# Gathering table rows by index without a bound on the indices

## The reference

```
h = feats * rsqrt(deg_out)[:, None]
m = segment_sum(h[src], dst, num_segments=n) * rsqrt(deg_in)[:, None]
x = (m @ W_gc + b_gc) + (feats @ W_res + b_res)
core = top-2 mixture of 64 experts, 256 -> 512 -> 256, over x
y = x + core
out = layernorm(feats + batchnorm(y) * gamma + beta)
```

## Time and profile before

| | |
|---|---|
| Median of 3 runs | 3077.5 us (3076.79 to 3083.35) |
| The profiled execution: its time | 3077.82 us |
| Its span, first to last instruction | 3076.0 us |
| Mean granted clock of TensorE | 0.826 of full speed |
| First and last start of a gather at L465 | 217.4 and 2259.5 us |
| First and last start of a gather at L490 | 2298.2 and 2863.2 us |

### The profile page before, as it was taken

How to read it: one execution, slowest core, us unless ns; L and a number is a source line. 1 busy time by engine, 2 the same in 40 slices (tenths; PEclk the granted TensorE clock), 3 DMA queues, 4 the chain that set the end, 5 groups by cost and what they waited for, 6 DMA issues and landing times.

```text
span 3076.0 us, 44225 instructions
## 1 busy us (share of the span) xinstructions
PE 2073.9 (67%) x10214; PEld 1715.2 (56%) x10263; DVE 1252.8 (41%) x3095; ACT 396.0 (13%) x1350; POOL 2030.9 (66%) x1989
## 2 busy tenths in 40 slices
PE   7955555565666666666667667677758898989370
PEld 7944344454444444555555555555647787989350
DVE  9971112122222333444444445555551222222467
ACT  1010000000000000000101111111112222322013
POOL 2017777777777777777777777777744677777603
PEclk6557877778788888888888899998988999999785
DMA  8033333333333333333333333333323465666332
GB/s 285 0 99 102 102 101 101 102 103 103 103 104 103 105 103 105 105 105 105 106 105 105 107 107 107 107 107 107 108 78 121 154 194 179 200 184 192 111 118 83
DMA packets 205321, 362.69 MB, mean 118 GB/s; under 512 B 43336, under 2 KB 126070, under 8 KB 205054
## 3 DMA queue, kind: packets, MB, share of 16 engines
q0 software_dynamic: 93888, 230.63, 26.0%
q1 hardware_dynamic: 104058, 123.31, 12.7%
q10 hardware_dynamic: 7108, 6.43, 0.6%
HBM read 328.57 MB, written 57.52 MB: 126 GB/s over the span
## 4 chain that ended last, share of the span: by engine, by line
POOL 45%; PE 21%; issue 19%; DVE 6%; DMA 4%; DVEq 2%; POOLq 1%; ACT 1%; PEld 1%; ACTq 0%; SPq 0%; PEldq 0%
POOL ring L465 22%; POOL stage L465 22%; PE bank L1270 7%; PE bank L1264 6%; PE bank L1135 3%; PE bank L1155 3%; DMA ring<-nodes,slots 2%; DVE acc L1048 1%; PE bank L1257 1%; DMA stage<-y 1%; PE bank L1195 1%; DVE stage L757 1%; PEld bank L1342 1%; PE bank L1174 0%; DVE srcT L1087 0%
## 5 line engine op out<-in xcount | busy, mean ns | idle before, releaser
L465 POOL DMA_INDIRECT ring<-table,ring_idx x792 | 790.8, 999 | 242.1 <-issue 240.9
L465 POOL DMA_INDIRECT stage<-table,ring_idx x776 | 774.5, 998 | 236.4 <-issue 235.2
L1155 PE MATMUL bank<-ring,hot 128*128 128x257 f32 x1056 | 310.4, 458 | 181.7 <-DMA ring<-table,ring_idx 166.1
L1155 PE MATMUL bank<-stage 128*128 128x257 f32 x1040 | 307.4, 460 | 166.3 <-DMA stage<-table,ring_idx 155.8
L1155 PEld LDWEIGHTS bank<-ring,hot 128*128 128x128 f32 x1056 | 241.2, 234 | 244.9 <-issue 158.2
L1155 PEld LDWEIGHTS bank<-stage 128*128 128x128 f32 x1040 | 238.8, 235 | 229.8 <-issue 155.1
L953 DVE TENSOR_TENSOR acc<-acc,bank 128x257 f32 x196 | 82.9, 423 | 614.8 <-PE bank L1155 577.5
L500 POOL DMA_INDIRECT y<-ring,slots x192 | 192.7, 1004 | 97.3 <-issue 57.6
L1155 PE MATMUL bank<-ring,stage 128*128 128x257 f32 x528 | 170.3, 493 | 118.6 <-DMA ring<-table,ring_idx 95.9
L1264 PEld LDWEIGHTS bank<-ring,stage 128*128 128x128 f32 x1984 | 237.0, 196 | 16.3 <-issue 11.7
L1264 PE MATMUL bank<-ring,stage 128*128 128x128 f32 x1984 | 241.0, 281 | 6.3 <-issue 3.6
(11 more groups left out here) (230 smaller groups left out, 2550.6 us busy)
## 6 DMA issues: line engine op xcount, KB each, us to landing
stage<-in_L_gnn_w_dram SPq DMA_DIRECT2D x128, 512.0 KB, 3.9
ring<-table,ring_idx POOLq DMA_INDIRECT x792
y<-zeros SPq DMA_DIRECT2D x49, 256.0 KB, 2.7
stage<-y SPq DMA_DIRECT2D x14, 896.0 KB, 7.3
stage<-table,ring_idx POOLq DMA_INDIRECT x776
stage<-in_L_gnn_b_dram SPq DMA_DIRECT2D x64, 128.0 KB
nodes<-yS ACTq DMA_DIRECT2D x49, 128.0 KB
xs<-in_x_dram SPq DMA_DIRECT2D x1, 6144.0 KB
```

The source lines that it names most:

```text
L465: pool.indirect_dma_start(out=ring(q)[:, j, 0:D], out_offset=None, in_=table[:, :], in_offset=bass.IndirectOffsetOnAxis(ap=ring_idx[:, q, ...
L1155: last = pe.matmul(bank[:, 0:D + 1], hots[:, j, :], ring(q)[:, j, :], start=j == 0, stop=j == CPG - 1)
```

## The change

The gathers at L465 lose their bound and the order to skip what is above it. All other indirect DMAs (L490, L500 and those of the extra chunks) keep theirs. The order of the instructions of all five engines, and what they wait for, is the same in both programs; what differs is the one register operand on each of the 1,568 gathers and the flag beside it.

```diff
                     for j in range(CPG):
                         pool.indirect_dma_start(
                             out=ring(q)[:, j, 0:D], out_offset=None, in_=table[:, :],
-                            in_offset=bass.IndirectOffsetOnAxis(ap=ring_idx[:, q, j:j + 1], axis=0),
-                            bounds_check=last_node, oob_is_err=False).then_inc(gath[q], 16)
+                            in_offset=bass.IndirectOffsetOnAxis(ap=ring_idx[:, q, j:j + 1], axis=0)).then_inc(gath[q], 16)
             gather(0, True)
             with pool.Fori(1, STEPS - 1) as it:
                 gather(it, False)
```

## The result

Over five runs each, the changed kernel takes 3005.77 us (2999.11 to 3007.82) and the kernel before 3076.79 us (3070.46 to 3083.35): a ratio of 0.9765, with a 95% interval from 0.9753 to 0.9777, or 71 us less. The forecast of no change was the wrong case of those listed; the time lies within the range and 9 us from the price of rival A at 0.06 us.

What follows compares the result with a forecast made beforehand. The prediction took POOL's back-to-back gathers at L465 to bound most of the gather stage. Its terms summed 0 - 0 + 0 = 0, so 3077 us, with a range for 8 in 10 from 2875 to 3105 us.

Steps and rivals of the forecast that it cites:

- forecast of no change: Whole kernel: same path, nothing to be seen, 3077 us with its own range of 3071 to 3084; chance 0.46.
- rival A: The test costs time in POOL's program, so L465 gathers get shorter: 2997 us at 0.06 us; chance 0.28 up to 0.15 us.
- What bounds the kernel: Gather stage: POOL issues gathers without waiting, 1.303 us per step, leading over about 1,356 of 1,568; PE follows except at the end.
- (1): L465 gathers: one register operand less for POOL's sequencer to read, hidden under the 0.30 us gap; taken as 0.
- (2): L465 gathers: the test of each index inside the instruction, taken as 0, with 0.06 and 0.15 us kept for the range.
- (3): End of the gather stage: 704 more padding rows fetched, 0.7 MB, within 3.9 us of cover; taken as 0.
- (4): Other engines: no instruction moves and none waits for anything new; no price, 0.
- The point from which it matters: L465 gathers: 0.2% or 6.2 us of the kernel, 4.6 ns per gather, is what a measurement can tell from no change.
- Rival B: Padding at the stage's end: 704 fetches of one row answered one behind the other, 30 us later, 3108 us; chance 0.08.

Runs made afterwards that it cites:

- experiments 3, 4, 8 and 9: Kernel before with half the rows skipped; with gathers of 128 to 16 rows; changed kernel with expert-stage bound dropped, empty slots fetching one row, 3020.1 us, or spread, 3014.13 us.

## Why the prediction was right or wrong

**What bounds the kernel: right.** POOL led the gather stage, and a gain of 52.5 ns per gather came through as 71 us of 82, 87%; I had 1,356 of 1,568, 86%. The rest is lost where I had it, at the end of the stage, but from group 160 on, which the kernel before reaches at 1895 us and not at 2100. Shorter gathers give up the lead sooner, so that the two shares agree so closely is in part luck.

**(1) The register operand at 0: right for the gap,** which stayed 0.30 us. I had taken for granted that the operand can cost nothing inside the instruction; whether part of the 52 ns is its price, no run separates.

**(2) The test inside the instruction at 0: wrong, and this is the step that failed.** I took "the value of the nearest row (skipped against fetched, no difference)". The row was true, and half of the rows skipped show it again; but it compares gathers that all have a bound. I had said so myself, and then took its value anyway. What the bound costs is 52 ns at 128 rows, close to the 0.06 us taken from the expert stage. That 0.06 was of another origin, since it is a spread between gathers which all have a bound; its nearness to the measured value is luck. Rival A, priced 2997 us, is what happened, at 0.28.

The mechanism that I named for it, a comparison that runs for each index, was off too: four fifths of the cost are the same at 16 and at 128 rows. The Trainium skill's page GPSIMD Engine Reference, section Performance pitfalls for Q7 kernels, has 2.03 cycles per element for a loop with compare and select, and 1.03 after unrolling. One cycle for each of 128 indices, 0.107 us, was my estimate from it; it would shrink to 0.013 at 16 rows. The runs have 0.052 and 0.042, so a cost per element doesn't describe this one.

**(3) The padding at 0: right as far as seen.** The queue moved 231.34 MB and not 230.63, 0.7 more. In the changed kernel PE was 19 us behind the last gather, so the cover was ample. From 2172 to 2184 us POOL's queue shows this:

```profile
q0 software_dynamic: 281, 0.76, 48.5%
```

Its last packet ended at 2181.5 us, 14 us before PE turned to that group at 2195.53. Rival B would have needed until 2170.3 + 41 = 2211 us.

**(4) The other engines: right** on the chip of the result. I hadn't considered that another engine leads on other chips.

**The point from which it matters** was 4.6 ns per gather; the cost was eleven times that. When so little decides, 0.46 for no change was too much for a cost of which no row existed.

## What to carry to other kernels

Where GpSimd issues indirect DMAs one behind the other and leads the chain, padding the table so that no index can leave it, and dropping the bound, saved 52 ns of 1,303 per gather; on a chip where another engine led it saved nothing, and the kernel was 1.6% slower. A row that shows two outcomes of a test to cost the same says nothing of the test itself: when every instance in the trace has the feature, its cost is unmeasured, and where 5 ns of 1,303 decide, as here, the larger chance belongs to "it costs something". And a gain that is tied to one leader should be confirmed on more than one chip.

## What was unexpected of the hardware

- An indirect gather's time on POOL is nearly all fixed: 849 ns for 16 rows and 946 for 128, without a bound. The cost of its bound is mostly fixed too: 42 ns at 16 rows, 52 at 128, and 16 ns more at 128 rows if exceeding it is an error.
- Skipping rows takes away their bytes and hardly any packets: with half of them skipped the queue moved 128.40 MB in 93,792 packets, against 231.34 MB in 93,888, and a gather took 998 ns as before.
- Rows that are all the same are slower to fetch than spread ones, but far from one after the other: about 0.03 us more of one engine's time per row, in 12,000 rows.
- The same program took 3077 us with the result and 3079 us on the chip of experiments 3, 4, 8 and 9, and 3796 and 3799 us on two other chips. POOL's gathers had the same length on all, within 2 ns. The traces from those two have long waits of DVE that the profile can't name; their cause is open.
